# Cross- and self-attention block: four edits to the order of work at the seams between stages

## The reference, cut to what matters

```python
# layer L0: cross-attention to a context of 77 tokens
xq  = ada_ln(x, cond, Wss_q);  xkv = ada_ln(ctx, cond, Wss_kv)
q = xq @ Wq + bq;  k, v = split(xkv @ Wkv + bkv)
x = x + softmax(q k^T / sqrt(32)) v @ Wp + bp
# layer L1
xn = ln(x) * (1 + scale_a) + shift_a
q, k, v = split(xn @ W_qkv + b_qkv)                                   # stage "qkv"
x = x + gate_a * (softmax(q k^T * scale) v @ W_proj + b_proj)         # stage "self": 512 x 512 scores a head
x = x + softmax((ln(x) @ W_qc) k_c^T * scale) v_c @ W_cproj + b       # stage "cross": 512 x 77 scores a head
x = x + gate_m * (gelu(modulate(ln(x)) @ W_mlp1 + b) @ W_mlp2 + b)    # stage "mlp"
```

## Time and profile before

| | |
|---|---|
| median of the three runs | 2545.93 us (2542.42 to 2553.80) |
| the profiled execution's own time | 2551.88 us |
| its span, first to last instruction | 2550.1 us |
| its mean granted TensorE clock | 0.973 |
| busy: PE / DVE / ACT / POOL | 94% / 55% / 40% / 23% |
| stretches: L0 150 to 500, qkv 550 to 820, self 821 to 1447, cross to about 1845, mlp to the end | us from the span's start |

### The profile page before, as it was taken

One profiled execution on the slowest core, in us unless ns is written; L12 is line 12 of the kernel. 1 busy time (PEld: TensorE's weight loads), 2 busy tenths in 40 slices (PEclk: granted clock), 3 DMA queues, 4 the chain that ended last, 5 costly groups with the idle time before them and its releaser, 6 DMA issues.

```text
span 2550.1 us, 32330 instructions
## 1 busy us (share of the span) xinstructions
PE 2408.3 (94%) x12048; PEld 1688.5 (66%) x12048; DVE 1390.8 (55%) x2463; ACT 1025.2 (40%) x1831; POOL 582.4 (23%) x325
## 2 busy tenths in 40 slices
PE   6889999999999899999998789999999999999999
PEld 5656666578877344444444457667588888888887
DVE  4566666654456777877777457666643222322221
ACT  3444444433322555555554334444442322233232
POOL 2101211210000466666665412111211011101100
PEclk9889999999999899999999899999999999999999
DMA  6687767555574546565553478787431101110110
GB/s 209 188 208 225 210 188 216 174 168 194 190 239 150 120 114 157 138 149 136 124 148 92 127 184 218 202 222 194 153 108 58 58 1 58 58 51 7 58 42 17
DMA packets 261323, 354.19 MB, mean 139 GB/s; under 512 B 61027, under 2 KB 109243, under 8 KB 261166
## 3 DMA queue, kind: packets, MB, share of 16 engines
q1 hardware_dynamic: 259998, 348.27, 48.4%
q0 software_dynamic: 1168, 3.85, 0.4%
HBM read 233.78 MB, written 116.69 MB: 137 GB/s over the span
## 4 chain that ended last, share of the span: by engine, by line
PE 81%; DVE 7%; ACT 4%; issue 3%; DMA 3%; SPq 1%; POOL 1%; DVEq 0%; ACTq 0%; POOLq 0%
PE banks L396 43%; PE banks L2195 14%; PE banks L1901 6%; PE banks L1923 4%; PE banks L1880 4%; PE banks L1935 2%; PE banks L1318 2%; PE banks L1332 2%; PE banks L1339 2%; PE banks L354 2%; DMA norm_x<-x 1%; ACT wide L377 1%; DVE negated_max L1815 1%; DVE norm_x L321 1%; PE banks L765 1%
## 5 line engine op out<-in xcount | busy, mean ns | idle before, releaser
L1979 ACT ACTIVATE self_exponentials<-banks 128x512 f32<-128x512 f32 x512 | 286.4, 594 | 291.2 <-PE banks L1935 138.7
L1815 DVE TENSOR_REDUCE negated_max<-banks 128x1 f32<-128x512 f32 x512 | 329.9, 677 | 100.4 <-PE banks L1880 98.9
L1781 POOL TENSOR_TENSOR self_exponentials<-self_exponentials,self_exponentials 128x2048 f32<-128x2048 f32 x64 | 294.5, 4602 | 202.5 <-ACT self_exponentials L1979 202.5
L2195 PE MATMUL banks<-mlp_w_down_hi,out_parts 128*128 128x512 f32 x1024 | 333.8, 389 | 0.1
L337 POOL TENSOR_SCALAR norm_rstd<-norm_mean_var 128x4 f32<-128x4 f32 x32 | 8.0, 249 | 1341.3 <-DVE norm_mean_var L316 1341.3
L2152 DVE TENSOR_TENSOR out_parts<-wide,out_parts 128x512 fp32r<-128x512 f32 x128 | 93.0, 727 | 371.2 <-ACT out_parts L2224 371.2
L2214 ACT ACTIVATE wide<-banks,bias_columns 128x512 f32<-128x512 f32 x128 | 88.3, 690 | 426.0 <-PE banks L396 426.0
L1901 PE MATMUL banks<-self_query_stack,self_key_stack 98*128 98x512 f32 x512 | 233.3, 457 | 7.8 <-ACT self_exponentials L1979 4.9
L1901 PEld LDWEIGHTS banks<-self_query_stack,self_key_stack 98*128 98x128 f32 x512 | 97.6, 191 | 185.9 <-ACT self_exponentials L1979 147.3
L2195 PEld LDWEIGHTS banks<-mlp_w_down_hi,out_parts 128*128 128x128 f32 x1024 | 192.2, 188 | 40.5 <-DVE cross_last_x_rows L1261 0.5
L1880 PE MATMUL banks<-self_key_stack,self_query_stack 96*128 96x512 f32 x512 | 208.6, 411 | 6.3 <-DVE negated_max L1815 5.1
(11 more groups left out here) (208 smaller groups left out, 5323.6 us busy)
## 6 DMA issues: line engine op xcount, KB each, us to landing
L_query_stack<-q_parts_L SPq DMA_DIRECT2D x96, 256.0 KB, 4.9
norm_x<-x SPq DMA_DIRECT2D x24, 1024.0 KB, 7.5
self_query_stack<-q_parts_self SPq DMA_DIRECT2D x96, 256.0 KB, 4.1
self_key_stack<-k_parts_self SPq DMA_DIRECT2D x96, 256.0 KB, 6.3
cross_query_stack<-q_parts_cross SPq DMA_DIRECT2D x96, 256.0 KB, 4.9
x_rows<-x SPq DMA_DIRECT2D x23, 1024.0 KB, 5.9
x<-x_rows SPq DMA_DIRECT2D x22, 1024.0 KB, 5.0
q_parts_L<-out_parts SPq DMA_DIRECT2D x32, 512.0 KB, 3.7
```

The costliest lines, as they stand in the source:

```text
L1781: e.tensor_tensor(self.p[kt - 1][:], self.p[kt - 1][:], self.p[kt][:], ALU.add).then_inc(self.paired.sem, 1)
L1815: e.tensor_reduce(k.nm[n % 2][:, h * NT + t:h * NT + t + 1], k.bank[:, self.max_banks.of["max", i], :], AX_X, ALU.max, negate=True).then_i ...
L1979: e.activation(self.p[kt][:, h, :], k.bank[:, self.scores.of["score", i], :], ACT.Exp, scale=SCALE).then_inc(self.exp.sem, 1)
L2195: mm = e.matmul(bank, l, w, start=j == 0 and q == 0, stop=j == JC - 1 and q == 2)
```

## The change

1. **First self group.** `maxima(2)` and `max_rows(1)` go from the first self group into the self prologue, which so has 51 steps in place of 35; qkv takes them from one batch earlier and two at a time in its last batch, and group 0 has no maxima.
2. **Last self pair.** POOL's last pair addition is dropped; PE sums both key tiles with ones itself (eight matmuls of 32x512 in place of four).
3. **Cross prologue.** Cross's first `load_diagonals` comes ahead of its query weights. Self takes (1, 5, 4, 8, 6) steps of cross in its last five groups, six in a `braid` with the last `finish` (made 6 rounds short in place of 15), and nine in a `braid` with the projection of batch 7, which has two banks (0, 1) in place of one.
4. **Layer norm turns, in L0 and cross.** The last quarter of a turn starts one round earlier (from group 4 of the query order on). In the groups with g = 1, maxima start one round later. The next stage's norm comes one group earlier: (1, 4, 4, 1, 4, 0) steps in the last six groups. The last batch's `add_base` comes behind group 30, where it was behind the next stage's steps.

```diff
@@ CrossAttention.run
-            return after(2, turning[b]) if g == 3 else None
+            return after(1 if n >= self.LEAD else 2, turning[b]) if g == 3 else None
...
         def splits():
+            if self.layer:
+                s.load_diagonals(0)
...
-        s.load_diagonals(0)
+        if not self.layer:
+            s.load_diagonals(0)
...
-            if n >= LAST - G - 1:
-                side.append(some((1, 4, 4, 4, 1)[n - LAST], following))
+            if n >= LAST - len(self.ahead):
+                side.append(some(self.ahead[n - LAST], following))
...
-                             s.maxima(n + self.MAX) if n + self.MAX < LAST else None,
+                             after(g == 1, s.maxima(n + self.MAX)) if n + self.MAX < LAST else None,
...
+            if n == LAST - 2:
+                s.add_base(B - 1)
         s.values(LAST - 1)
         yield from s.finish(LAST - 1)
         yield from some(self.tail, following)
-        s.add_base(B - 1)
         yield from s.project(B - 1)
@@ Qkv.run
-                if b >= B - 2:
-                    weave(some(b - B + 3, following))
-                elif b == B - 3 and m == G:
+                if b >= B - 3:
+                    weave(some(2 if b == B - 1 else 1, following))
+                elif b == B - 4 and m == G:
                     next(following)
...
-                if b >= B - 2 and (b < B - 1 or t < 2):
-                    weave(some(b - B + 3, following))
+                if b >= B - 3:
+                    weave(some(2 if b == B - 1 else 1, following))
...
-            if B - 5 < b < B - 2:
+            if B - 6 < b < B - 3:
@@ SelfAttention
+    AHEAD = (1, 5, 4, 8, 6)
...
+        yield from braid(s.maxima(2), after(4, s.max_rows(1)))
...
-            yield from braid(s.attend(n), s.finish(n - 1) if n else None, s.maxima(n + self.MAX) if n + self.MAX < LAST else None,
-                             after(2, s.max_rows(n + self.ROWS)) if n + self.ROWS < LAST else None, *side)
+            yield from braid(s.attend(n), s.finish(n - 1) if n else None, s.maxima(n + self.MAX) if 0 < n < LAST - self.MAX else None,
+                             after(2, s.max_rows(n + self.ROWS)) if 0 < n < LAST - self.ROWS else None, *side)
...
-        yield from s.finish(LAST - 1)
-        yield from some(5, following)
+        yield from braid(s.finish(LAST - 1), some(6, following))
         s.add_base(B - 1)
-        yield from s.project(B - 1)
+        yield from braid(s.project(B - 1), some(9, following))
@@ sum_pair of TensorE
-            pe.wait_ge(*self.paired(2 * n + j))
+            if 2 * n + j < 2 * LAST - 1:
+                pe.wait_ge(*self.paired(2 * n + j))
+                tiles = (2 * j,)
+            else:
+                pe.wait_ge(*self.exp((n * NT + NT - 1) * GH + GH - 1))
+                tiles = (2 * j, 2 * j + 1)
```

More of the change, by code:

```diff
@@ L1607 @@
     attend: object = idle(GH * NT)
-    finish: object = idle(15)
+    finish: object = idle(6)
     project: object = idle(4 * NT)
@@ L1825, in finish @@
         def finish(n):
-            for _ in range(10):
+            for _ in range(self.finish_steps(n) - 5):
                 yield
@@ L1943, in project @@
                 pe.wait_ge(*self.w.ready(self.wp_at + KC - 1))
-                bk, before = self.products.take(("project", i), self.gated(i))
+                bk, before = self.project_ring(b).take(("project", i), self.gated(i))
                 if before:
@@ L1992, in finish @@
             e.copy(k.o_wide[n % 2][:], k.bank[:, self.heads.of["heads", n], :]).then_inc(self.heads_copied.sem, 1)
-            for _ in range(12):
+            for _ in range(self.finish_steps(n) - 3):
                 yield
```

31 lines of the change are left out of this document (18 added, 13 removed).

## The result

| | before | with the change |
|---|---|---|
| median of nine runs each, us | 2545.93 | 2536.61 |
| lowest and highest | 2539.96, 2558.12 | 2532.49, 2538.70 |
| the profiled execution's own time | 2551.88 | 2532.49 |
| its mean granted clock | 0.973 | 0.983 |

The ratio to before is 0.9959, with a 95% interval of 0.9942 to 0.9976: faster by 0.4%, some 10 us, where 47 were forecast. The measured median lies above the range's upper end of 2534.

A forecast was written before the change was run, and what follows sets the result against it. TensorE, busy 94% of the span, was taken as the bound, leaving its idle time and missing clock to win. The terms summed to -47 from 2551.9, giving 2505 profiled, 2499 us on the median's scale; range 2472 to 2534.

The forecast's parts named there:

- Steady cross: Where batches meet in cross, the moved rounds take away 5.5 of 6.1 us of PE's waits.
- the delayed maxima: In 14 g = 1 places of L0 and cross, maxima a round later cost 0.3 us each, +4.
- rival D: In g = 1 groups, late maxima stall PE and the clock falls: slower, 2572 us; chance 0.07.
- L0's waits: Where batches meet in L0, 11 of 13.9 us of PE's waits go, mainly on ring and maximum.
- rival C: At meetings of batches the gaps only move, PE waiting for whatever is last: 2540 us; chance 0.11.
- L0's clock: Where batches meet in L0, closing gaps brings back 10 of 15.1 us of missing clock.
- Rival A: In L0 the clock does not come back, so its 10 us are not won: 2509 us; chance 0.22.
- Tail of self: From self's end into cross's prologue, fewer waits and half the missing clock win 20 us.
- End of L0: Additions for batch 7 moved earlier remove the first wait and half the second, winning 5 us.
- First self group: Self's first group falls from 17.4 to 10 us without its maxima, less qkv's 3.65: 3.5 us won.
- The baseline: Whole kernel: the profiled execution was 5.95 us above the median, so the forecast went from 2505 to 2499.
- B: At self's tail a braided step waits behind another, so 7 instead of 20 us go: 2512 us; chance 0.15.

The follow-up runs named there:

- e1: The changed kernel with maxima in the g = 1 groups not delayed; 2521.84 us, ratio 0.9911 to the kernel before.
- e3: The changed kernel with the turn's last quarter two rounds late as before, maxima still delayed; 2535.96 us, ratio 0.9972 to the kernel before.
- e4: The changed kernel with both the early turn and the delayed maxima undone in L0 and cross; 2532.28 us, ratio 0.9954 to the kernel before.
- e9: The changed kernel without delayed maxima, early turn in L0 alone, whole self tail as before; 2534.28 us, ratio 0.9950 to the kernel before.
- e6: The changed kernel without delayed maxima, early turn in L0 alone, last add_base behind the tail again; 2523.35 us, ratio 0.9929 to the kernel before.
- e7: e6 with the next stage's norm where it was before the change; 2523.79 us, ratio 0.9923 to the kernel before.
- e8: The changed kernel without delayed maxima, early turn in L0 alone, first self group as before; 2521.54 us, ratio 0.9921 to the kernel before.

## Why the prediction was wrong

**The sum, term by term.** Forecast -47; the two traces show -19.4, the medians -9.3.

- *Steady cross, -5.5: wrong in sign.* Cross from its first to its last sums became 10.6 us longer, and this one term, 16 us off, is the largest error. The step that failed is the price of the delayed maxima: 0.3 us in each of 14 places, +4, with the reason that the steady stages show no such wait. They could not show it, because the delay is what makes it. The count of 14 and the price of rival D, 1.77 a place, were the right kind of thing. Measured, PE's waits on maxima in these groups are 0.6 us a place in L0 (3.5 in six, at L1308) and 11.5 us in the seven of cross (2.86 and 8.61 in the table's six), 1.6 a place; the clock fell behind the first of them alone. What I had not looked at is what stands ahead of the maxima in DVE's program in the round where they go: the norm's statistics, with their wait for the DMA of the rows. I also set the transposition of the maxima two groups on; with `MAX` = 3 and `ROWS` = 2 it stands in the next group, so the margin from which the round was taken was smaller than I thought. And the early turn, for which I took -5.5, brought nothing in cross: its gains on `out_parts` and `x_lo` went into the wait on the heads. The two edits were costed one by one; e1, e3 and the change show 3.4, 0.9 and 7.5, so that they are no sum. How they work together is not shown. In groups 3 to 27 DVE's waits for the DMA of the rows are up to 5.12 us with both edits, 3.81 with the delay alone (e3), 4.45 with the turn alone (e1) and 1.08 before, which points at the statistics again.
- *L0's waits, -11: measured -3.* The ring's wait went, and another came for the same ring (L354 on the heads, 4.6), and the maxima's. This was rival C, "the ring, the maximum and the query copy come within 1 us of each other", right for the waits and not for the clock.
- *L0's clock, -10: about right.* It is the source of the gain: all windows at meetings at 1.00, and L0 10 us shorter by e4 against e1, 8.6 of it PE's work. Between the two traces of before and the change it is 13.4 of 15.4. The sum in time of both terms is so -10 where -21 stood, and the trace of before flattered it by another 4.5. Rival A, that the clock would stay, fell.
- *Tail of self, -20: measured -13.9 in the traces,* 10 in the medians (e9). It lay between its bounds of 7 and 30. The clock came back by half as I took it (0.87 to 0.93 over the stretch), but it was worth less than the 6.0 of the sum: PE's busy time fell by 2.8 us, with 0.9 us of new work in it. A window's length times (1 - clock) counts idle time too, and in the tail PE stood still for almost a quarter of the time. The waits were mis-sized, 11 us of idle time for the 15.5 that I took: x's low parts still cost 4.3 where I had nothing left, and `heads_parts` took 2.5.
- *End of L0, -5: measured +1.4, or nothing that the whole shows by e6 and e7.* I had the row that warned of it: a POOL addition beside DVE, and the rule on the port. I applied both to self, where nothing came of it, and not to the end of L0, where the same `add_base` was moved into a full group, beside four DVE instructions with both operands in SBUF. The 3.09 went and 4.13 came.
- *First self group, -3.5: measured 0.* The group was to be 10 us and was 15.7, with 9.48 of them ACT's as counted, but 12.27 of PE work, where the earlier trace rows less the maxima already said 14.73 - 3.65 = 11.1, and the DMA engines at 0.94 of their time, against 0.74 before. qkv's price of 3.65 was right (e8: 4.0).
- *The baseline.* I subtracted 5.95 to come to the median, as if the profiled execution were slow evenly. Some 4.5 of the 6 us were, by e4, the clock at L0's meetings, thus a part of what the change removes; I counted it in the terms, and in the subtraction again.

With the measured sizes the terms are +11 for cross, -10 for L0, -10 to -14 for the tail and about nothing for the rest: -9 to -13, about the measured -9.3.

**The range and the chances.** It missed by 2.6 us. All cases but C and D stood on the same sum. The upper end held 12 us of D's waits, but as an extra to A and B, and no case had cross longer than before. With the measured 11.5 us in cross's seven places in place of 2.1 the forecast would have stood at -38 and the range's upper end at 2543, which holds the measured time; the other terms were too large still. Rival D asked for 3.4 us a place before the kernel is slower, but below that point it still eats the gain, and the range must hold that.

**Which signs held.** The clock near 1.00 at the meetings, `wide` gone, no wait on the diagonals or the pair: yes. The waits on the maximum in g = 1, named as the sign of D: yes, at L1308 of 0.6 each, with larger ones in cross at the maxima's own matmuls. The 77 us from group 30 to cross's first scores, from 97: no, some 84. From the mark of self's group 28 to these scores it is 121.4 us before and 108.8 with the change, 12.6 less. Waits at the end of L0 under 4: no.

## What to carry to other kernels

When an edit moves a step by a round, read what stands ahead of it then in the program of the engine that consumes it, and what that waits for in its turn, not how long the step waits now. Here that was a DMA, and PE's wait grew with it from 0.6 to 3.3 us. Two such moves in the same rounds have to be costed together. A clock that is missing while the engine stands still costs nothing: price it by the engine's busy time, not by the window. Where the clock falls at a seam in one execution and not in another, its price in one profile is not the kernel's: compare it with a second order that keeps the seam, before it is put into the sum.

Try the parts of a change alone. Here one line of it cost more than the whole won, and about half of its edits moved nothing that the medians show.

## What the runs showed that I had not expected

With the same order at a meeting, the granted clock was 1.00 at the first two meetings of e4 and 0.72 and 0.86 by turns at the other four; at the four shown PE worked for 10.47, 10.45, 10.76 and 10.46 us of 12. The gaps are the same too: 0.74, 0.92 and 0.63 us at the second meeting, where the clock held, 0.75, 0.92 and 0.63 at the third, where it fell. With the chunk moved by a round and PE's waits only 3 us less in six batches, it held in all eleven profiles. What decides it, the place of the gap or something outside the kernel, stays open; no run varied the gap by itself.

POOL's additions and DVE: with four additions of 1.6 us back to back, DVE's operations on two operands in SBUF went from 0.7 to between 1.60 and 1.81 us, four in a row, and the wait reached PE by way of ACT as 4.13 us in this profile, and as 1.0 to 3.5 in nine others with the early additions. Taking it away was worth nothing that the medians show (e6).
